# Re-ordering the software pipeline of the last stage (convolution, mixture of experts, feed-forward) of a one-core kernel

## The reference, cut to what matters

```python
h = _layernorm(x, axis=-1) * (1 + cb) + sb
x = x + gb * _L1_ffn_ref(h, ...)

def _forward(x, ...):                        # E, TOPK, K = 8, 2, 3; HID = 32
    xc = depthwise_conv(x, dw_kernel) + dw_bias          # 3 taps, causal
    xc = silu(einsum('bdl,ed->bel', xc, pw_w) + pw_b)
    x1 = x + transpose(xc)
    logits = einsum('bsd,ed->bse', x1, router_w) + router_b
    top_v, top_i = lax.top_k(logits, 2)
    top_w = softmax(top_v)
    rw = sum(one_hot(top_i, 8) * top_w[..., None], axis=-2)
    ye = silu(einsum('bsd,eod->bseo', x1, expert_w) + expert_b)
    combined = einsum('bse,bseo->bso', rw, ye)           # all 8 experts, gated
    moe_out = einsum('bsd,od->bso', combined, out_w) + out_b
    h = rmsnorm(x1 + moe_out, norm_w)
    ff = gelu(einsum('bsd,hd->bsh', h, ff_down_w) + ff_down_b)
    return h + einsum('bsh,dh->bsd', ff, ff_up_w) + ff_up_b
```

## Time and profile before

| what | value |
|---|---|
| median of 3 runs | 1032.95 us (1030.37 to 1036.62) |
| the profiled execution: time, span | 1030.37 us, 1028.5 us |
| busy of the span: PE, DVE, ACT, POOL | 82%, 72%, 61%, 50% |
| mean granted TensorE clock over the span | 0.903 of full |
| last stage | from about 846 us to the end |

### The profile page before, as it was taken

One profiled execution on the slowest core, in us unless ns is written; L12 is line 12 of the kernel. 1 busy time (PEld: TensorE's weight loads), 2 busy tenths in 40 slices (PEclk: granted clock), 3 DMA queues, 4 the chain that ended last, 5 costly groups with the idle time before them and its releaser, 6 DMA issues.

```text
span 1028.5 us, 14161 instructions
## 1 busy us (share of the span) xinstructions
PE 839.7 (82%) x4604; PEld 464.3 (45%) x4604; DVE 744.7 (72%) x1590; ACT 630.4 (61%) x1099; POOL 518.0 (50%) x816
## 2 busy tenths in 40 slices
PE   4569999999989888888868999999723748987986
PEld 3212222222222222222456877777622526766774
DVE  5488888878788878782358777777649886958772
ACT  1128787878766777576456777777515635545672
POOL 3253464646445666345273067776779416653221
PEclk9669999999998999798598999999966887989997
DMA  6474636373635364202113166667250000000000
GB/s 198 93 177 135 156 117 156 117 155 117 155 117 130 96 185 98 109 23 99 49 42 126 62 235 231 211 242 243 88 228 0 1 0 1 1 1 11 21 21 31
DMA packets 44308, 109.98 MB, mean 107 GB/s; under 512 B 7422, under 2 KB 20222, under 8 KB 38726
## 3 DMA queue, kind: packets, MB, share of 16 engines
q1 hardware_dynamic: 38172, 96.75, 31.9%
q0 software_dynamic: 4992, 10.36, 3.0%
q10 hardware_dynamic: 1072, 1.98, 0.7%
HBM read 57.65 MB, written 51.03 MB: 106 GB/s over the span
## 4 chain that ended last, share of the span: by engine, by line
PE 53%; DVE 22%; ACT 8%; issue 7%; POOL 5%; DMA 3%; SPq 1%; another core or an unknown queue 1%; ACTq 0%; POOLq 0%; DVEq 0%
PE PS L1041 11%; DVE mx L866 7%; PE PS L1030 7%; PE PS L320 5%; PE PS L318 5%; PE PS L319 4%; PE PS L1014 4%; ACT E L787 2%; PE PS L996 2%; DVE XC L1735 2%; DMA HT<-xs 1%; PE PS L985 1%; ACT ov L793 1%; PE PS L1481 1%; DVE cb L2151 1%
## 5 line engine op out<-in xcount | busy, mean ns | idle before, releaser
L866 DVE TENSOR_REDUCE mx<-PS 128x2 f32<-128x1024 f32 x256 | 305.5, 1220 | 86.5 <-PE PS L1014 79.6
L787 ACT ACTIVATE E<-PS 128x512 f32<-128x512 f32 x512 | 277.0, 599 | 86.6 <-PE PS L1030 83.6
L1030 PE MATMUL PS<-Q,K 51*128 51x512 bf16 x512 | 168.2, 402 | 7.9 <-ACT E L787 4.3
L1014 PE MATMUL PS<-K,Q 48*128 48x512 bf16 x512 | 141.4, 409 | 25.1 <-DVE mx L866 23.9
L1041 PE MATMUL PS<-E,V 128*9 128x512 f32 x1024 | 143.4, 634 | 19.2 <-ACT ov L793 18.6
L1232 POOL DMA_INDIRECT yd<-yt,goes x92 | 96.7, 1051 | 35.7 <-issue 23.9
L1030 PEld LDWEIGHTS PS<-Q,K 51*128 51x128 bf16 x512 | 37.1, 95 | 159.7 <-ACT E L787 93.9
L1385 DVE TENSOR_TENSOR Gl<-Gf,Gh 128x512 fp32r<-128x512 f32 x116 | 81.1, 701 | 31.8 <-ACT Gh L1266 27.3
L509 POOL DMA_INDIRECT xs<-HT,pos x64 | 63.9, 998 | 76.3 <-ACT E L787 47.9
L1260 ACT ACTIVATE Gf<-PS,WR 128x512 f32<-128x512 f32 x92 | 63.4, 690 | 38.4 <-PE PS L320 30.7
L2151 DVE SCALAR_TENSOR_TENSOR cb<-ye,gt,cb 128x128 f32<-128x128 f32 x224 | 65.3, 365 | 0.0
(11 more groups left out here) (400 smaller groups left out, 1919.2 us busy)
## 6 DMA issues: line engine op xcount, KB each, us to landing
WR<-wsd SPq DMA_DIRECT2D x23, 1028.0 KB
xs<-zero SPq DMA_DIRECT2D x8, 2112.0 KB, 8.1
wsd<-wsp SPq DMA_DIRECT2D x8, 1024.0 KB, 4.1
Q<-dqk SPq DMA_DIRECT2D x16, 384.0 KB, 5.6
HT<-xs SPq DMA_DIRECT2D x23, 264.0 KB
dqk<-SPL SPq DMA_DIRECT2D x30, 192.0 KB, 2.8
K<-dqk SPq DMA_DIRECT2D x15, 384.0 KB
stage<-in_w SPq DMA_DIRECT2D x9, 516.0 KB
```

The costliest lines, as they stand in the source:

```text
L787: e.activation(E[:, m % 4, n % 4], PS[:, bank["exp", n], :], ACT.Exp).then_inc(*k.inc("exp", n))
L866: e.tensor_reduce(mx[:, 2 * s % 96:2 * s % 96 + 2], PS[:, o:o + 2, :], AX.X, ALU.max, negate=True).then_inc(*k.inc("max", s))
L1014: return e.matmul(PS[:, o + n % 2, :], Q[r, b % 3, h // 2, qt * P:(qt + 1) * P], K[r, b % 3, h // 2, :], start=True, stop=True)
L1030: e.matmul(PS[:, o, :], K[r, b % 3, h // 2, kt * P:(kt + 1) * P], Q[r, b % 3, h // 2, :], start=True, stop=True).then_inc(*k.inc("exp_mm", n))
```

## The change

In the orders of the four engines of `ffn1()`: three groups of the choice in place of four (tiles 0 to 3, 4 to 15, 16 to 31), chosen before pass 0 and in passes 3 and 7, with tanh in passes 0, 3, 8 and gates in 0, 3, 8. DVE's combine is moved to the end of a pass, and low, x1l, logits, choice, gates, bn_out and final stand before it. On TensorE hr moves between the two experts of the odd pass, fd to the end of that pass, and fo to the even pass after it, one pass earlier than before. ScalarE follows: the hr copy between the silus of the odd pass, gelu at its end, norm at the end of the even pass, tanh behind silu. All loops are one pass shorter. What each piece computes is the same.

```diff
--- before.py
+++ after.py
@@ -1900,8 +1900,7 @@
             D.close()
             flat = lambda t: t.rearrange("p a n -> p (a n)")
             HEAD, NP = 1, 2 * NB
-            GROUP = {0: (0, 4), 1: (4, 8), 2: (8, 16), 3: (16, NT)}
-            CHOICE = {0: 0, 2: 1, 4: 2, 8: 3}
+            GROUP = {0: (0, 4), 1: (4, 16), 2: (16, NT)}
             group = lambda b: next(g for g, (a, c) in GROUP.items() if a <= 4 * b < c)
             lng = lambda b: next(g for g, (a, c) in LNG.items() if a <= 4 * b < c)
             front = {p: p + HEAD for p in range(NB - HEAD)}
@@ -1971,7 +1970,7 @@
                 z(1)
                 x1(0)
                 pool_ln_group(e, k, 2)
-                for p in range(NP + 6):
+                for p in range(NP + 5):
                     if p + 1 in front:
                         z(front[p + 1])
                     if p == 0:
@@ -2067,30 +2066,30 @@
                 z(1)
                 silu(0)
                 x1h(0)
-                for p in range(NP + 6):
+                for p in range(NP + 5):
                     if p in front:
                         hidden(front[p])
-                    if p % 2 and 0 <= p // 2 - 2 < NB:
-                        norm(p // 2 - 2)
-                    if p % 2 == 0 and 0 <= p // 2 - 3 < NB:
-                        hr(p // 2 - 3)
                     if p < NP:
                         expert(2 * p)
-                    if p in CHOICE:
-                        tanh(CHOICE[p])
                     if p + 1 in front:
                         z(front[p + 1])
                     if p - 1 in front:
                         x1h(front[p - 1])
+                    if p % 2 and 0 <= p // 2 - 2 < NB:
+                        hr(p // 2 - 2)
                     if p < NP:
                         expert(2 * p + 1)
                     if p in front:
                         silu(front[p])
+                    if p in (0, 3, 8):
+                        tanh((0, 3, 8).index(p))
                     if p % 2:
                         if 0 <= p // 2 - 1 < NB:
                             turned(p // 2 - 1)
-                    elif 0 <= p // 2 - 3 < NB:
-                        gelu(p // 2 - 3)
+                        if 0 <= p // 2 - 2 < NB:
+                            gelu(p // 2 - 2)
+                    elif 0 <= p // 2 - 2 < NB:
+                        norm(p // 2 - 2)
 
             def dve(e, k):
                 def low(b):
@@ -2171,23 +2170,26 @@
                 logits(0)
                 best(0)
                 second(0)
-                for p in range(NP + 6):
-                    if p and p in CHOICE:
-                        best(CHOICE[p])
-                        second(CHOICE[p])
-                    if p - 1 in CHOICE:
-                        gates(CHOICE[p - 1])
-                    if p % 2 == 0 and 0 <= p // 2 - 2 < NB:
-                        bn_out(p // 2 - 2)
+                for p in range(NP + 5):
                     if p in front:
                         low(front[p])
-                    if 1 <= p <= NP:
-                        combine(p - 1)
                     if p - 1 in front:
                         x1l(front[p - 1])
                         logits(front[p - 1])
-                    if p % 2 and 0 <= p // 2 - 3 < NB:
-                        final(p // 2 - 3)
+                    if p == 0:
+                        gates(0)
+                    if p in (3, 7):
+                        best(1 + p // 7)
+                        second(1 + p // 7)
+                    if p in (3, 8):
+                        gates(1 + p // 8)
+                    if p % 2 == 0:
+                        if 0 <= p // 2 - 2 < NB:
+                            bn_out(p // 2 - 2)
+                        if 0 <= p // 2 - 3 < NB:
+                            final(p // 2 - 3)
+                    if 1 <= p <= NP:
+                        combine(p - 1)
 
             def pe(e, k):
                 uses = []
@@ -2293,18 +2295,18 @@
                         if 0 <= p // 2 - 2 < NB:
                             out(p // 2 - 2)
                         if 0 <= p // 2 - 3 < NB:
-                            fd(p // 2 - 3)
-                    elif 0 <= p // 2 - 3 < NB:
-                        fo(p // 2 - 3)
+                            fo(p // 2 - 3)
+                    elif 0 <= p // 2 - 2 < NB:
+                        hr(p // 2 - 2)
                     if p < NP:
                         expert(2 * p + 1)
                     if p in front:
                         pw(front[p])
                     if p % 2:
-                        if 0 <= p // 2 - 2 < NB:
-                            hr(p // 2 - 2)
                         if 0 <= p // 2 - 1 < NB:
                             ct(p // 2 - 1)
+                        if 0 <= p // 2 - 2 < NB:
+                            fd(p // 2 - 2)
 
             return pe, dve, act, pool, sp
 
```

## The result

The changed kernel is slower: ratio 1.0088 to the kernel before on the same chip, 95% interval 1.0065 to 1.0109 (medians 1039.9 and 1032.6 us; these two alone are 0.7% apart, inside the interval). Forecast were 1042 us and slower by 0.9%.

What follows compares the result with a forecast made beforehand. TensorE and DVE bound the front, TensorE with gaps the steady part, a dependent chain the end. 1.0 + 2.85 + 5.9 - 1.85 + 1.75 = 9.65 us on 1030.4 gave 1040.0; median 2.6 above, so 1042; range 1031 to 1050.

Steps and rivals of the forecast that it cites:

- Passes 0 to 4: Last stage up to norm(0): +1.0 us (-1.2 to +3.1), later combine(2) and silu(5) against a dropped top-2.
- the unknown: gates(1) on DVE beside GpSimd's tensor_scalar: about 1 us of waiting taken, 0 and 2.8 for the range.
- Passes 5 to 7: From norm(0) to pass 8: +2.85 us (+1.4 to +4), TensorE waiting at hr(0) and hr(1) with an expert behind.
- the listed pieces: TensorE's work from norm(0): hr, expert 11, pw(6), ct, fd, zt, expert, route, out(1), fo(0), expert, pw(7), 18.55 us.
- The price of an expert at the low clock: An expert on TensorE after a gap takes 3.4 us instead of 1.9, by the doubling that fo was said to show.
- Passes 8 and 9: +5.9 us (+3.6 to +7): 20.4 us against 14.5, combine(6) and gates(2) late on DVE, TensorE waiting for norm(2).
- DVE's new order: Passes 8 and 9: combine(6) behind x1l(7), logits and top-2; bn_out(2) behind tanh(2) and gates(2); +5.9 us.
- Passes 10 to 15: Steady part: -1.85 us (-5.3 to 0), gelu wait gone, period 14.25 us against 14.48 before.
- the ring: Passes 10 to 15: fo, final, combine, silu, hr copy, fd, expert, out, 14.25 us against 13.2 of matmul.
- level: Rival, about 1031 us, chance 0.23: no DVE backlog; passes 8 and 9 about +1, steady part wins 5, rest about 4.
- The end: After the last expert: +1.75 us (+0.5 to +3.5), combine(15) waits behind final(5), out(7) at +12.65 instead of +10.9.
- the one large term: The term for passes 8 and 9, called the dear step: +5.9 us, 20.4 us for two passes against 14.5.

Runs made afterwards that it cites:

- a: Changed kernel with combine(6) and combine(7) before x1l, top-2, gates and bn_out on VectorE; passes 8 and 9 21.0 us, ratio 1.0099.
- b: Changed kernel with bn_out ahead of the choice and the gates on VectorE; passes 8 and 9 18.7 us, ratio 1.0106.
- c: Changed kernel with the edits of both a and b; passes 8 and 9 13.6 us, ratio 1.0034.
- d: Changed kernel with final behind combine on VectorE in every even pass; passes 10 to 15 39.7 us, ratio 1.0064.
- e: Changed kernel with the edits of c and d together; stage 179.8 us, ratio 1.0002.
- h: e with hr(0) and hr(1) behind the pass's second expert and pw on TensorE, their copies behind silu; passes 5 to 7 30.3 us, ratio 1.0013.
- second pair: Kernel before and changed kernel each traced once more, unedited; stages 179.0 and 186.2 us, changed kernel's ratio 1.0101.
- f: Kernel before with only the moves on TensorE and ScalarE, its own four groups, VectorE order and tanh place; passes 8 and 9 13.4 us, ratio 1.0004.
- g: Changed kernel with four groups of the choice again, combine still last; passes 8 and 9 14.3 us, ratio 1.0013.

## Why the prediction was right, step by step

*Passes 0 to 4: +1.0 forecast, -2.7 in the first pair of traces, -1.5 in the second.* Both are below the term's own range (-1.2 to +3.1), but it can't be settled from two pairs. Eight traces run the same program up to norm(0) (changed twice, a to e, h) and have 64.4 to 69.8 us here, mean 66.2; the two of the kernel before have mean 66.5. Up to expert 16, where seven of them (without h) differ by no more than a combine, a bn_out or a final moved within a pass, they have 94.5 to 100.7, mean 97.1, against 95.0 and 94.6. Of the step's inner points one held: combine(2) ended 52.5 us into the stage, against 47.0 before. gates(1), the unknown, took 1.0 us in all, so of the about 1 us of waiting in the term nothing came. It ran late in GpSimd's tensor_scalar. An operation of the same kind early in it, the one at 898.23, took 0.68 us instead of 0.26, and the kernel before has such a row as well (a two-input operation of 0.97 us at 894.73), which the forecast didn't look at when it took the one at 896.99. What held combine(2) up beside its new place was not gates(1) but shift(1), beside which its first two operations took 1.51 us, where 0.47 is usual. DVE, then GpSimd:

```profile
898.23 0.68 DVE L377 TENSOR_TENSOR wk<-wk 128x96 f32<-128x96 f32 x1
...
899.58 0.26 DVE L2130 TENSOR_TENSOR wk<-wk 128x96 f32<-128x96 f32 x1
...
900.41 1.51 DVE L2147 TENSOR_SCALAR cb<-ye,gt 128x128 f32<-128x128 f32 x2
```

```profile
897.76 2.78 POOL L1960 TENSOR_SCALAR FUG<-FUG 128x1024 f32<-128x1024 f32 x1
900.51 1.32 POOL L1950 TENSOR_TENSOR X<-X,GA 128x512 f32<-128x512 f32 x1
```

*Passes 5 to 7: +2.85 forecast, +2.5 measured* (1.3 in the second pair, just below the range; the changed kernel's 30.2 and 30.1 stood still, the kernel before moved). TensorE waited 5.8 us at hr(0), with the low clock behind it, and worked through the listed pieces; norm(1) ended 25.5 us after norm(0) (25.2 forecast). The price of an expert at the low clock, 3.4 us, was not what the rows of fo give (0.77 to 0.49 is a factor of 1.6, not 2); the three that were meant took 3.6 (expert 11), 3.0 (15) and 3.1 (19).

*Passes 8 and 9: +5.9 forecast, +5.9 measured,* 20.4 in both. combine(6) ended at 35.8 (35.7 forecast), VectorE waited 3.7 us for tanh (3.9), TensorE 5.5 for norm(2) (5.6). Two chains, one through combine(6) and the buffers, one through tanh(2) and the gates, are both in the forecast's walk, and it let the second end last. The cause is shown by a, b, c, f and g. The forecast called it "DVE's new order"; g narrows this to the place of the last group's top-2 and gates.

*Passes 10 to 15: -1.85 forecast, -1.5 measured.* Period 14.29 (14.25). d shows the ring. The lower bound of the term, -5.3, was too far: the forecast's own sum has two periods, and with 13.2 in place of 14.25 it gives -3.95. With the ring cut (d, e) the stretch gained 3.1 against before; hr's wait of 0.28 us for norm in each period is most of what is left. The rival *level*, which took 5 for this part, was too hopeful by the same step.

*The end: +1.75 forecast, +2.1 measured* (3.1 in the second pair). combine(15) started 7.1 us after the last expert, as forecast. fd(6), now between ct(7) and out(7), ran at the lower clock in addition, so that out(7) came at 12.8 us, not 12.65.

The stage is thus 6.2 us longer in the first pair and 7.2 in the second, where 9.65 was forecast. In the first pair the first term makes the difference (3.7 us); in the second it and passes 5 to 7 fall short by 2.5 and 1.5, and the end is 1.35 above its term. The timed runs say 9.1 us (0.88% of 1032.6), with an interval from 6.7 to 11.3, and their medians are 7.4 apart; the traces' 7.2 is inside it.

So the direction and the size come from the one large term, whose mechanism and length were both right. That the total agrees to a tenth of a percent is in part luck: the first term, +1.0, isn't borne out by either pair of traces, its sign is open within 2 or 3 us, and the end and passes 5 to 7 each moved by 1 us between the two pairs.

## What to carry to other kernels

In a hand-ordered pipeline, walk each queue for the operations that wait for another engine and ask what stands behind them: here the five small operations of the gates, behind a tanh, held back statistics whose input had been ready for 5.9 us, and through them TensorE. When two chains of nearly equal length end at the same engine, undoing one shows little or nothing; test both together before a cause is ruled out. And a move that shortens one wait (gelu before fo) can close a ring through three engines; add up the ring before counting the gain.

## What the runs showed of the hardware

VectorE beside GpSimd: a two-input VectorE operation of 128x96 took 0.26 us late inside GpSimd's 2.78 us tensor_scalar (899.58, above), and one earlier in it took 0.68 us (898.23). That one ended 1.15 us after the tensor_scalar began. In the second trace of the changed kernel and the two of the kernel before an operation of this kind is stretched at the same place and ends 1.16, 1.12 and 1.11 us after that start. The row of the kernel before:

```profile
894.73 0.97 DVE L373 TENSOR_TENSOR wk<-wk,p 128x64 f32<-128x64 f32 x1
```

So VectorE doesn't wait out this GpSimd operation, but in its first 1.1 to 1.2 us it does wait; why is not shown. Two tensor_scalars of VectorE took 1.51 us instead of 0.47 with the two-input operation of shift(1) beside them.

An idle spell of TensorE can be paid again after it. After 5.5 us of waiting expert 19 took 3.1 us in the changed kernel, start to start, where 1.9 is its time at 2.4 GHz, and the mean granted clock of passes 8 and 9 was 0.83 there (0.92 in its second trace, with the same length of 20.4 us) against 1.00 in c. Not every wait costs this: after 2.4 us in front of pw(5), at 906.37, the same trace has nine matmuls in 2.2 us, which is full speed.
